# Bias products on quarters of the TensorE array, with a fixed selecting column, in a transformer layer with routed experts

## The reference, cut to what matters

```python
scores = xf @ gate_w + gate_b            # 625 tokens, 768 numbers each
topv, topi = jax.lax.top_k(probs, 3)     # expert 0 is shared, 3 of the others are chosen
h = jnp.einsum('td,edh->eth', xf, fc1_w) + fc1_b[:, None, :]     # 768 -> 1536
h = jax.nn.gelu(h, approximate=False)
h = (h - mu) * jax.lax.rsqrt(var + LN_EPS) * ln_w[:, None, :] + ln_b[:, None, :]
y = jnp.einsum('eth,ehd->etd', h, fc2_w) + fc2_b[:, None, :]     # 1536 -> 768
out = jnp.einsum('te,etd->td', combine, y)
```

## Time and profile before

| | |
|---|---|
| median of 3 runs | 1200.68 us (1199.53 to 1201.06) |
| profiled execution | 1206.77 us, its span 1205.1 us |
| PE busy | 1151.7 us (96%) |
| DVE, ACT, POOL busy | 761.0 (63%), 659.1 (55%), 490.4 us (41%) |
| granted TensorE clock, mean | 0.979 |
| bias products, L1911 | 3 of 512 and 2 of 384 columns a block |
| scatters, L795 | 27, mean 4.68 us on POOL |

### The profile page before, as it was taken

How to read it: one execution, slowest core, us unless ns; L and a number is a source line. 1 busy time by engine, 2 the same in 40 slices (tenths; PEclk the granted TensorE clock), 3 DMA queues, 4 the chain that set the end, 5 groups by cost and what they waited for, 6 DMA issues and landing times.

```text
span 1205.1 us, 20725 instructions
## 1 busy us (share of the span) xinstructions
PE 1151.7 (96%) x6465; PEld 1014.8 (84%) x6493; DVE 761.0 (63%) x1191; ACT 659.1 (55%) x1040; POOL 490.4 (41%) x340
## 2 busy tenths in 40 slices
PE   6999999999889999999999999999999999999985
PEld 5999898777666678888999988888889989998874
DVE  7862643256487656525866865747675896666973
ACT  3222673155500145336876684857776977486953
POOL 1188888788811000443632521312443642222511
PEclk8999999799999999999999999999999999999988
DMA  9030005140300330146596574565775959377933
GB/s 311 17 88 2 3 2 142 26 163 2 82 13 3 104 116 28 27 116 212 223 350 231 188 291 148 207 205 187 300 272 204 373 183 336 86 279 282 349 115 98
DMA packets 63089, 191.71 MB, mean 159 GB/s; under 512 B 14316, under 2 KB 15383, under 8 KB 63045
## 3 DMA queue, kind: packets, MB, share of 16 engines
q1 hardware_dynamic: 51316, 172.86, 39.3%
q0 software_dynamic: 11728, 18.27, 8.5%
HBM read 178.74 MB, written 15.09 MB: 161 GB/s over the span
## 4 chain that ended last, share of the span: by engine, by line
PE 81%; DVE 5%; ACT 4%; DMA 4%; issue 3%; POOL 1%; ACTq 0%; SPq 0%; DVEq 0%; another core or an unknown queue 0%; POOLq 0%
PE banks L1939 25%; PE banks L1923 23%; PE banks L1672 5%; PE banks L1689 4%; PE banks L1739 3%; PE banks L1837 3%; PE banks L1859 3%; PE banks L1704 3%; PE banks L1907 3%; PE banks L1761 2%; PE banks L1911 2%; DMA out<-ysb,sidx 2%; ACT kfeat L1432 2%; PE banks L1900 1%; PE banks L1750 1%
## 5 line engine op out<-in xcount | busy, mean ns | idle before, releaser
L731 POOL DMA_INDIRECT edge_dram<-epair,eslot x165 | 224.4, 1360 | 99.4 <-issue 99.4
L795 POOL DMA_INDIRECT out<-ysb,sidx x27 | 126.3, 4679 | 233.1 <-issue 198.6
L521 ACT ACTIVATE w2hi<-w2raw 128x1536 fp32r<-128x1536 f32 x96 | 139.1, 1483 | 90.2 <-DMA w2raw<-in_L_ffn_fc_w 80.0
L534 DVE TENSOR_TENSOR w2lo<-w2raw,w2hi 128x1536 fp32r<-128x1536 f32 x96 | 164.5, 1753 | 25.9 <-ACT w2hi L521 23.8
L1939 PE MATMUL banks<-w2hi,hthi 128*128 128x384 f32 x624 | 161.8, 340 | 0.1
L1939 PE MATMUL banks<-w2hi,htlo 128*128 128x384 f32 x624 | 159.2, 336 | 0.0
L1939 PE MATMUL banks<-w2lo,hthi 128*128 128x384 f32 x624 | 158.9, 335 | 0.0
L521 ACT ACTIVATE w1hi<-w1raw 128x1536 fp32r<-128x1536 f32 x96 | 137.6, 1495 | 29.2 <-DMA w1raw<-in_L_ffn_fc_w 25.7
L534 DVE TENSOR_TENSOR w1lo<-w1raw,w1hi 128x1536 fp32r<-128x1536 f32 x80 | 144.1, 1865 | 0.0
L1923 PE MATMUL banks<-w1hi,xthi 128*128 128x512 f32 x486 | 139.7, 396 | 2.6 <-POOL w1lo L534 2.6
L1923 PE MATMUL banks<-w1lo,xthi 128*128 128x512 f32 x486 | 136.9, 390 | 0.0
(11 more groups left out here) (347 smaller groups left out, 1867.8 us busy)
## 6 DMA issues: line engine op xcount, KB each, us to landing
w1raw<-in_L_ffn_fc_w SPq DMA_DIRECT2D x96, 768.0 KB
w2raw<-in_L_ffn_fc_w SPq DMA_DIRECT2D x96, 768.0 KB, 6.6
xs<-in_x SPq DMA_DIRECT2D x10, 336.0 KB
edge_dram<-epair,eslot POOLq DMA_INDIRECT x165
wg<-in_L_gnn_W SPq DMA_DIRECT2D x1, 2304.0 KB, 12.6
wv<-in_L_mix_W_qkv SPq DMA_DIRECT2D x1, 2304.0 KB, 13.8
wk<-in_L_mix_W_qkv SPq DMA_DIRECT2D x1, 2304.0 KB, 17.7
wq<-in_L_mix_W_qkv SPq DMA_DIRECT2D x1, 2304.0 KB, 9.0
```

The costliest lines, as they stand in the source:

```text
L521: act.activation(unit(w2hi if second else w1hi, second, u), unit(w2raw if second else w1raw, second, u), ACT.Copy).then_inc(w2_hi if secon ...
L534: eng.tensor_tensor(unit(w2lo if second else w1lo, second, u), unit(w2raw if second else w1raw, second, u), unit(w2hi if second else w1hi, ...
L731: pool.indirect_dma_start(out=edge_dram, out_offset=bass.IndirectOffsetOnAxis(ap=eslot[:, k:k + 1], axis=0), in_=epair[:, k, :].bitcast(I3 ...
L795: pool.indirect_dma_start(out=out, out_offset=bass.IndirectOffsetOnAxis(ap=sidx[:, 0:1], axis=0), in_=ysb[:, :], in_offset=None, bounds_ch ...
```

## The change

1. Each bias is kept as two float32 parts instead of three bf16 parts. The 16 + 16 rows of both parts fill one quarter of 32 partitions. Quarters 0, 1 and 2 hold the three thirds of the hidden bias, quarter 3 the first half of the output bias, and quarter 0 holds its second half in further columns. A bias product takes 32 rows.
2. The stationary operand is a fixed column of a new tile `sel_now`: column 0 for the hidden bias, column 1 for the output bias. POOL copies the columns of the experts into it, once each iteration (`select_after`), when the last bias product that reads it is done (`biased`). PE waits for `sel_ready` at the head of each iteration of the loop, and before the last output bias.
3. The output bias product now opens the sum of the second layer instead of closing it. In the loop it stands right behind the hidden bias, ahead of `turn_x`, and the wait for `y_ok` moves there too. In iterations 1 to 3 and for the last block it stands just ahead of `fc2`.
4. `weigh` waits for `w2_used` (6 j + 12) instead of `fc2_ok`.
5. Ahead of the loop: POOL no longer clears `bsplit` but makes eight selects instead of three, DVE splits the biases in two operations instead of five, SP reads the table back in ten transfers instead of six, and PE waits for these before its first `fc1`.

The diff, cut to its core:

```diff
-            for g in range(3):
+            for g in range(128 // E):
                 pool.wait_ge(sel_ok, g + 1)
...
+            pool.wait_ge(sel_ok, 1 + 128 // E)
+            pool.sem_inc(sel_ready, 6)
+
+            def select(n, e):
+                pool.tensor_copy(sel_now[:, n:n + 1], selw[:, bass.ds(e, 1)]).then_inc(sel_ready, 1)
+
+            def select_after(j, e, e_next):
+                pool.wait_ge(biased, j + 1)
+                select(0, e_next)
+                select(1, e)
+
+            select(0, 0)
+            select(1, 0)
...
             with pool.Fori(NT, rest) as j:
                 with_first(pool, j, low_beside_gelu(j))
+                select_after(j, entry(pool, EXPERT, j, E - 1), entry(pool, EXPERT, j + 1, E - 1))
                 gather_after(j)
                 scatter(j)
                 take_slots(j + 1)
...
             def weigh(j):
 
-                act.wait_ge(fc2_ok, j)
+                act.wait_ge(w2_used, C * j + 2 * C)
...
-            def bias(ps, e, a, b):
-                return pe.matmul(ps, selw[:, bass.ds(e, 1)].broadcast_to([128, 128]), bsplit[:, a:b],
-                                 start=False, stop=True)
-
-            def fc1(j, e, beside={}):
+            def bias(ps, n, group, column, first):
+
+                width = ps.shape[-1]
+                a = 32 * group
+                return pe.matmul(ps, sel_now[a:a + 32, n:n + 1].broadcast_to([32, 128]), bsplit[a:a + 32, column:column + width],
+                                 start=first, stop=not first)
+
+            def hidden_bias():
+
+                for n in range(3):
+                    last = bias(hid_ps[n][:, :], 0, n, 0, False)
+                    last.then_inc(fc1_ok, 1)
+
+            def out_bias():
+
+                bias(y_ps[0][:, 0:384], 1, 3, 0, True)
+                return bias(y_ps[1][:, 0:384], 1, 0, 512, True)
+
+            def fc1(j, e, beside={}, with_out=False):
...
-                for n in range(3):
-                    bias(hid_ps[n][:, :], e, 512 * n, 512 * n + 512).then_inc(fc1_ok, 1)
+                hidden_bias()
+                if with_out:
+                    pe.wait_ge(y_ok, j)
+                    out_bias().then_inc(biased, 1)
...
-                bias(y_ps[0][:, 0:384], e, F, F + 384)
-                bias(y_ps[1][:, 0:384], e, F + 384, F + D).then_inc(fc2_ok, 1)
...
+                pe.wait_ge(sel_ready, 2 * j)
+                turn_and_enter(j, e, with_out=True)
+                leave(j, e_before, with_out=True)
```

More of the change, by code:

```diff
@@ L275, in gps_kernel @@
         eslot = at("eslot", s0 + 1344, [TP, ET], U32)
-        bsplit = small("bsplit", [128, F + D], BF16)
+        bsplit = small("bsplit", [128, 512 + 384], F32R)
+        s0 += 1024
         projt = at("projt", s0, [128, M])
@@ L449, in gps_kernel @@
             "fc1_ok gelu_ok ln_own ln_ok h_turned v_scaled hthi_ok htlo_ok")
[L450 removed]
+        y_ok, sidx_ok, scattered = sems("y_ok sidx_ok scattered")
         def done(eng, key):
@@ L641, in _, with bias_rows @@
             sp.wait_ge(st_bias, 32)
-            sp.wait_ge(bsplit_zero, 1)
-            for g in range(3):
-                sp.dma_start(bsplit[32 * g:32 * g + E, 0:F], bias1_dram[g, :, :]).then_inc(ld_eb, 16)
-                sp.dma_start(bsplit[32 * g:32 * g + E, F:F + D], bias2_dram[g, :, :]).then_inc(ld_eb, 16)
+            def bias_rows(group, column, of):
+                for half in range(2):
+                    a = 32 * group + E * half
+                    sp.dma_start(bsplit[a:a + E, column:column + of.shape[-1]].bitcast(F32), of[half, :, :]).then_inc(ld_eb, 16)
+            for group in range(3):
+                bias_rows(group, 0, bias1_dram[:, :, 512 * group:512 * group + 512])
+            bias_rows(3, 0, bias2_dram[:, :, 0:384])
+            bias_rows(0, 512, bias2_dram[:, :, 384:D])
             done(sp, ("pj", NT - 1, 1))
@@ L753, in _ @@
             pool.memset(selw[:, :], 0.0).then_inc(sel_ok, 1)
-            for g in range(3):
+            for g in range(128 // E):
                 pool.wait_ge(sel_ok, g + 1)
-                pool.affine_select(out=selw[:, :], in_=selw[:, :], compare_op=ALU.not_equal, fill=1.0, base=-32 * g, pattern=[[-1, E]], channel_multiplier=1).then_inc(sel_ok, 1)
+                pool.affine_select(out=selw[:, :], in_=selw[:, :], compare_op=ALU.not_equal, fill=1.0, base=-E * g,
+                                   pattern=[[-1, E]], channel_multiplier=1).then_inc(sel_ok, 1)
+            pool.wait_ge(sel_ok, 1 + 128 // E)
[8 more added lines that the diff above has]
+            select(1, 0)
             pool.iota(biota_i[:, :], [[1, TW]], base=0, channel_multiplier=0)
@@ L1960, in _ @@
                 taken(pe, ("gnn", 2, s))
-            pe.wait_ge(sel_ok, 4)
-            pe.wait_ge(ld_eb, 96)
+            pe.wait_ge(sel_ready, 8)
+            pe.wait_ge(ld_eb, 160)
             fc1(0, 0, {2: lambda: gate(2), 4: lambda: turn_xn2(3)})
+            pe.sem_inc(biased, 1)
             gate(3)
@@ L1966, in _, with turn_and_enter, leave @@
             messages(4)
-            def turn_and_enter(j, e, beside={}):
+            def turn_and_enter(j, e, beside={}, with_out=False):
                 pe.wait_ge(xtlo_ok, j + 1)
                 turn_h(j)
-                fc1(j, e, beside)
-            def leave(j, e_before):
+                fc1(j, e, beside, with_out)
+            def leave(j, e_before, with_out=False):
                 pe.wait_ge(v_scaled, j)
                 turn_x(j + 1)
-                pe.wait_ge(y_ok, j)
+                if not with_out:
+                    pe.wait_ge(y_ok, j)
+                    out_bias().then_inc(biased, 1)
                 fc2(j, e_before)
@@ L2003, in turn_last @@
                 turn_h(nb)
-            turn_and_enter(end, E - 1)
-            pe.wait_ge(y_ok, end)
+            pe.wait_ge(sel_ready, 2 * end)
+            turn_and_enter(end, E - 1, with_out=True)
             fc2(end, entry(pe, EXPERT, end - 1, E - 1), beside={END_TURN_AT: turn_last})
             pe.wait_ge(y_ok, nb)
+            pe.wait_ge(sel_ready, 2 * nb)
+            out_bias()
             fc2(nb, E - 1, endhi, endlo)
```

29 lines of the change are left out of this document (13 added, 16 removed).

## The result

The changed kernel takes **1207.6 us** (median of 4 runs, 1204.56 to 1210.52), the kernel before beside it 1200.87 (1199.53 to 1201.47). The ratio is 1.0046, with a 95% interval of 1.0026 to 1.0066: slower by 0.46%, where 1205.2 was forecast. The profiled execution of the changed kernel is the 1204.56 one, its span 1202.8.

The account below looks back on a forecast made before the run. TensorE was taken to bound the expert loop. First wait +1.2, clock +2.65, iterations 20 to 24 -1.3 and tail +2.0 sum to +4.5 us, on the median 1200.68: 1205.2 us, range 1195.5 to 1209.5.

Parts of the forecast that it names:

- Sum: Whole program: 1.2 + 2.65 - 1.3 + 2.0 = +4.5 us, giving 1211.3 profiled and 1205.2 for the runs.
- Bias products: PE in the expert loop: 0.99 us removed, one visit of the divided array 0.73 added, gain 0.26 an iteration.
- The copies: POOL's two copies behind the w1lo split: each ends with a DVE split, the second at 979.5 in iteration 19.
- The first wait: Head of iteration 20: PE idles over 6 us for the copies; first layer starts at 977.4 instead of 976.22, +1.2.
- The clock: After PE's first wait: 5.3 us at the 1.2 GHz level, costing half of that, +2.65 us.
- The tail: From iteration 25 to the end: late copies, half-clock turn, last turn later; next product at 1180.8, +2.0 us with the last visit.
- The anchor: Reference time: the profiled execution, 1206.77, stands 6.1 above the runs' median 1200.68, so the forecast was set to the median.
- Rival 3: Loop heads: POOL's copies are ready before PE, so faster, -4.7 to 1196.0, or 1194; chance 0.21.

Follow-up runs that it names:

- one_group: scalar_copies with all five quarter products on the same 32 rows of the array: iteration 28.12 us, 1207.68 us (1 run).
- two_visits: scalar_copies with the output's two quarter products back between turn_x and the second layer, apart from the hidden ones: iteration 27.90 us, 1200.64 us (1 run).
- second trace: Trace of the changed kernel run once more without alteration, on the same chip as its variants: 1208.8 us, ratio 1.0061.
- four_copies: Changed kernel with two further POOL copies, into a tile that nothing reads, ahead of the two PE waits for: 1210.66 us, ratio 1.0107.
- scalar_copies: Changed kernel with the two copies made by ACT instead of POOL, PE's wait still at the head of the iteration: 1195.06 us, ratio 0.9965.
- wait_only: Kernel before, with its own bias products, plus only the two POOL copies and PE's head wait for them: 1211.6 us, ratio 1.0108.
- late_wait: Changed kernel with PE's wait for the copies moved from the iteration's head to just ahead of the hidden bias products: 1193.95 us, ratio 0.9956.
- selects_first: Changed kernel with the two POOL copies put ahead of POOL's w1lo split instead of behind it: 1198.86 us, ratio 0.9992.
- scalar_late: Changed kernel with both the copies on ACT and PE's wait just ahead of the hidden bias: 1194.35 us, ratio 0.9950.

## Why the prediction was right

The forecast was 1205.2 us, and 1207.6 came, with PE's two waits as its cause. The mechanism is the one forecast; that the sum came so close is in part luck, since terms that were off cancelled (see **Sum**). Its steps:

- **Bias products.** Forecast 27.50 us an iteration, measured 27.50. The parts are as put: 0.09 into the divided array, 0.34 from the first quarter product to the fifth (0.10 and 0.23 put), 0.26 from there to the turn (0.17 and 0.09 put), and 0.06 for the transposes' weights (0.05 put). The overlap of four, taken from two halves, was worth 0.63, and one_group gave 0.62. The estimate by the Trainium skill's 3.07 times (TensorE: Matmul & The Clock Gate, "Measured speedup vs the span model"), a gain of 0.19 in place of 0.26, is not what this trace shows. Separate visits were priced 0.38 dearer than one (0.56 and 0.55 against 0.73) and cost 0.40 (two_visits). Iterations 1 to 3, put at 0.12 longer each, were 0.16, 0.27 and 0.09 longer in the second trace.
- **The copies.** "A small POOL copy ends when a DVE split does", one split for each: shown by the traces of the changed kernel and of four_copies. The rule of the Trainium skill (SBUF — State Buffer, "SBUF: two separate sides") agrees: 1.7 us beside a split on POOL, 0.24 at most on ACT.
- **The first wait.** Forecast over 6 us of idle time, measured 6.48 (3.52 in the second trace). From turn_h of iteration 1, the kernel was to be 3.5 us early at the head of iteration 19 and some 3.6 late at the head of 21 (the 3.8 less one iteration's gain); it was 0.8 early (504.45 against 505.29 us) and 4.6 late (567.62 against 563.06). The lead is mis-sized by two things: a stretch of half clock in iteration 1 (granted clock 0.53 from 451.90 to 455.50, where it is 1.00 at that place in the second trace), which was 33.14 us long, where it is 31.5 to 31.7 in six of the eight other traces with quarters and 33.1 and 33.2 in the other two, and the wait at iteration 17, where "in most iterations POOL is through in time" failed: a copy of 1.6 us, 0.77 of PE's wait, and an iteration longer by 0.93. Without waits (scalar_copies) the lead at 19 was 3.4 us.
- **The clock.** That 2.65 us go to the 1.2 GHz level was too much for the profiled execution: iteration 20 took 29.02 us, 1.5 over 27.50. The price was read from the earlier trace rows, where PE was busy all the time; here the low stretch began at 967.4, while PE still waited, and PE worked in 3.15 of its 6.9 us. In the second trace PE was back sooner and worked in 5.98 of them, and iteration 20 took 30.35, 2.85 over (busy time by stretch, PE first, granted clock behind the engines):

```profile
968.20:975.10 6.90, 5.98 (x20) 5.27 (x21) 6.90 (x5) 3.41 (x10) 5.75 (x4) 0.51 0.48 177
```

So the cost is half of what PE works at the lower level (1.6 and 3.0 us by this count, 1.5 and 2.85 measured). wait_only and four_copies agree: PE worked in 2.77 and 5.56 us of their low stretches, and iteration 20 was 1.4 and 2.7 us over. Idle time that falls into the stretch costs nothing more.
- **The tail.** Forecast +2.0, measured +1.4: 3.5 us late at the head of 25 (677.56 against 674.10), 4.9 at the end. The wait (5.67), the turn at 2.79, and the last turn at full clock are as put. The last visit starts at 1176.88, 1.6 later than the last products did before in the same count (1.8 put). The visit itself was put at 0.55 for 0.34, so 0.2. Its two products are on different quarters and start together, and the next product starts 0.37 after them (1177.25); at the end the old two products (0.34) are gone: 0.03 in place of 0.2. The end behind the last weighing is 0.2 shorter, for no reason that the rows show.
- **Sum.** Forecast +4.5, +4.9 in the profiled execution, +6.7 in the medians (and +8.6 when repeated). In the profiled execution the errors nearly cancel: the lead that was missing at iteration 19 adds 2.7, the two iterations behind it took 1.8 less than put (1.1 of it the clock), and the tail 0.6 less. The profiled executions of this kernel, 1204.56 and 1205.25, are among its shorter ones; others took up to 1210.6. What those wait for has no trace. More waits like that at iteration 17 (1.03 us in the second trace) are a candidate; it stays open.
- **The anchor.** The forecast was made against the kernel before's profiled time and then set to its median, 6.1 lower. That was right: the surplus goes with 20 us at half clock far ahead of the loop, a stretch that no other trace has at that length.
- **Rival 3** gave 1196.0, or 1194, for a kernel in which the copies never hold PE. That kernel is late_wait, 1193.95, and scalar_copies, 1195.06. The price of this rival was right within 2 us. Its condition, a scatter's issue that ends some 7 us sooner, did not hold in the changed kernel: 13.8 and 13.5 us at iteration 19 in its two traces. It did in late_wait's (1.9 us) and selects_first's (3.0), so at 19 it differs from one execution to the next; at 25 the issue took 13 us or more in every trace.

## What to carry to other kernels

Put a wait where its value is used, not at the head of the stage: the same two late copies cost 12 to 14 us at the head (ratios of 1.0046 and 1.0061 against late_wait's 0.9956), and nothing that could be measured where the bias is added (1193.95 us, and 1195.06 with the copies on ACT). If a small piece of work must be done in time, keep it off an engine that another one can lock out for a whole long instruction, and count such a piece as one instruction of the other engine each, however small it is. Moving such a piece ahead of the work that delays it helps only as far as what stands in front of it is in time: selects_first came back to the kernel before's time and no further. Small products on quarters of the array pay when they share one visit; in two visits they were slower than the whole-array products that they replaced.

## What the runs showed that I had not expected

- An idle time too short to matter by itself can bring the 1.2 GHz level, and need not. 1.95 us in the earlier trace rows did not; in scalar_late 2.09 us at the same place did: the first products behind it ran at half speed, 1.54 us for three in place of 0.98. That iteration took 31.42 us, where scalar_copies with a wait of 1.93 us took 29.68.

```profile
967.46 1.54 PE L1959 MATMUL banks<-w1hi,xthi 128*128 128x512 f32 x3 [2.09 <-POOL w1lo L536]
```

- A faster stage ahead of a fixed one turns into waiting. The changed kernel was at turn_h of iteration 1 some 7 us before the profiled execution of the kernel before, for reasons of the clock, though 10.58 us of what it had gained stood in a wait. In the chain DVE's `oh`, for which PE waits, stands behind POOL's 165 scatters of edges (L738), and these make up 18% of the chain in the page:

```profile
332.17 2.30 PE L1841 MATMUL banks<-oh 128*125 128x125 bf16 x16 [10.58 <-DVE oh L983]
...
PE 61%; POOL 19%; issue 7%; DMA 5%; DVE 4%; ACT 1%; SPq 0%; POOLq 0%; ACTq 0%; DVEq 0%
PE banks L1957 25%; PE banks L1975 24%; POOL edge_dram L738 18%; DMA out<-ysb,sidx 3%; PE banks L1927 3%; PE banks L1879 3%; PE banks L1920 2%; PE banks L1934 1%; DVE oh L983 1%; PE banks L1857 1%; PE banks L1692 1%; PE banks L1841 1%; DMA w2raw<-in_L_ffn_fc_w 1%; DMA xn_dram<-xn 1%; DMA xs<-in_x 1%
```

- The runs of a kernel with late copies at the head spread more in most cases, though not in all. The kernel before spreads over 5.1 us (17 runs, 1197.51 to 1202.62) and 3.9 (11 runs on another chip); with PE's head wait on POOL's copies it was 4.9 (wait_only, 4 runs), 6.0, 8.1, 6.9 (selects_first, 10 runs) and 14.9 (four_copies, 6 runs), with the later wait 2.2 and with ACT's copies 2.3 (5 runs each), with both 3.8. The counts of runs differ, and what the long runs wait for is not shown.
